# A twelve-stage transformer kernel on one core: six steps of lead instead of five in the last attention, and an earlier context load in the first stage

## The reference

```
# layer 0, attention (the first stage), 4 batches x 16 heads of width 128
x = x + softmax(mask(Q K^T / sqrt(128))) V Wo        # Q, K, V from layernorm(x), with biases
# beside it, for later stages: ternary and int8 versions of weights, and
# the context ctx scaled by its largest absolute value and rounded to fp8

# layer 3, cross attention (the last attention): self and cross heads, 4 x (16 + 16) of width 128
ln = layernorm(layernorm(x)) ; q, k, v = fp8(ln / s) W
q, k = layernorm over each head ("rows") ; P = softmax(q k^T / sqrt(128)) ; o = P v
out = fp8(concat(o) / smooth) Wproj
```

## Time and profile before

| | us |
|---|---|
| median of three runs | 2484.09 (2479.33 to 2488.4) |
| the profiled execution | 2485.58, its span 2483.8 |
| first stage with attention | about 24 to 345 |
| last attention | about 1618 to 2265 |
| mean granted TensorE clock | 0.899 |

### The profile page before, as it was taken

The page is one execution under the profiler, slowest core; times in us unless marked ns, Lnnn a source line. Parts: engine busy times, 40 slices in busy tenths (PEclk is TensorE's granted clock), DMA queues, the critical chain, the costliest instruction groups (busy, mean ns, idle before and its releaser), DMA issues. The chain is left out here.

```text
span 2483.8 us, 38355 instructions
## 1 busy us (share of the span) xinstructions
PE 2070.6 (83%) x13521; PEld 1473.3 (59%) x13521; DVE 1616.2 (65%) x4140; ACT 1109.7 (45%) x2507; POOL 874.7 (35%) x1388
## 2 busy tenths in 40 slices
PE   6898966798798469995559899959999999997991
PEld 4787843465464235553236576637878877785671
DVE  3775657444455945564757897858888888876333
ACT  2256642232342533432754755425555555553330
POOL 2147752112111311111000000046766767764444
PEclk9999987798898568997579999979999999998996
DMA  6014430000000030000000000041111111106553
GB/s 250 25 67 141 148 121 1 1 2 2 1 1 1 27 147 2 1 2 36 1 0 1 1 1 1 1 163 40 55 39 39 56 39 39 48 31 225 111 138 103
DMA packets 57693, 130.96 MB, mean 53 GB/s; under 512 B 6656, under 2 KB 23552, under 8 KB 55520
## 3 DMA queue, kind: packets, MB, share of 16 engines
q1 hardware_dynamic: 52656, 115.80, 13.6%
q0 software_dynamic: 4560, 12.46, 2.3%
q10 hardware_dynamic: 288, 0.26, 0.0%
HBM read 100.31 MB, written 26.08 MB: 51 GB/s over the span
## 5 line engine op out<-in xcount | busy, mean ns | idle before, releaser
L1270 ACT ACTIVATE K<-ps 128x768 f32<-128x768 f32 (+1 forms) x128 | 110.5, 864 | 164.7 <-PE ps L1086 162.9
L2792 POOL TENSOR_TENSOR K<-K 128x512 f32<-128x512 f32 x128 | 134.5, 1050 | 138.5 <-DVE K L2589 138.4
L2191 DVE TENSOR_TENSOR_SCAN W<-W,ps 128x512 f32<-128x512 f32 x128 | 155.8, 1217 | 42.0 <-issue 24.5
L2143 PEld LDWEIGHTS ps<-K 128*128 128x128 f32 x1024 | 136.8, 196 | 65.7 <-issue 51.9
L2732 ACT ACTIVATE K<-ps,K 128x256 f32<-128x256 f32 x128 | 60.6, 474 | 243.1 <-DVE K L2573 243.1
L2584 DVE TENSOR_SCALAR K<-ps,K 128x128 f32<-128x128 f32 x384 | 130.9, 403 | 35.1 <-POOL K L2809 34.8
L2143 PE MATMUL ps<-K 128*128 128x128 f32 x1024 | 139.2, 280 | 8.1 <-DVE W L2191 8.1
L1308 POOL CAST K<-K 128x8 bf16<-128x8 f32 x64 | 14.6, 229 | 369.8 <-issue 209.9
L2778 POOL TENSOR_SCALAR K<-K 128x1 f32<-128x1 f32 x16 | 3.6, 224 | 372.6 <-DVE K L2639 369.7
L2162 PE MATMUL ps<-W,C 128*128 128x512 f32 x256 | 133.3, 603 | 0.7 <-DVE W L2199 0.6
L2482 PE MATMUL ps<-K 128*128 128x256 f32 x512 | 131.8, 380 | 0.7 <-ACT K L2751 0.7
(11 more groups left out here) (528 smaller groups left out, 5849.4 us busy)
## 6 DMA issues: line engine op xcount, KB each, us to landing
W<-split_weights SPq DMA_DIRECT2D x32, 768.0 KB, 4.4
split_weights<-W SPq DMA_DIRECT2D x40, 384.0 KB, 2.6
W<-in_m SPq DMA_DIRECT2D x32, 256.0 KB, 4.9
results<-K SPq DMA_DIRECT2D x63, 128.0 KB
W<-split_weights SPq DMA_DIRECT2D x1, 5376.0 KB, 16.7
W<-in_wproj SPq DMA_DIRECT2D x16, 256.0 KB, 3.0
W<-in_m SPq DMA_DIRECT2D x32, 128.0 KB, 5.1
W<-split_weights SPq DMA_DIRECT2D x1, 3072.0 KB, 20.5
```

Source lines behind the costliest of these rows:

```text
L1270: e.activation(to, made, ACT.Exp, scale=self.SCALE).then_inc(*self.up("exp"))
L2143: m = e.matmul(ps[1 + 2 * (n % 2)][:, b * 128:(b + 1) * 128], self.dtuT[h][:, i, b * 128:(b + 1) * 128], self.diag[s % 4][:, b * 128:(b + ...
L2191: e.tensor_tensor_scan(self.st[i % 3], self.a[i % 3], ps[1 + 2 * (i % 2)][:, :], 0.0, ALU.mult, ALU.add).then_inc(*sig.up("m scan"))
L2792: e.tensor_tensor(Pv, Pv, st[:, 4:6].unsqueeze(2).to_broadcast([128, 2, 256]), ALU.mult).then_inc(*sig.up("x scaled"))
```

## The change

In the first stage the context load goes to the head of SP's list, behind the copy L407 ("lane spread") and ahead of the four stores of ternary weights, into the columns 2048 to 4095 of the shared area; SP no longer waits for the int8 weights, and its part is no longer spread over steps. GpSimd, which now writes the scaled context to columns 0 to 2047, takes over that wait. The work behind the fourth lane sum is spread over three steps: the sum in step 9, L332 and the small VectorE operations in step 10, L334 and L407 in step 11.

In the last attention `LEAD` is 6, the first step is -25 instead of -26, a prep tile takes four steps instead of five, and the feed-forward norms start at 94, 102 and 110. The two turns of prep tiles and of feed-forward inputs stand in steps with `s % 4 == 3` (3 and 7 of a batch; 99, 103, 107, 111, 115, 119). Rows of unit `s + 4` are turned in step `s`. So with `s % 4` = 0, 1, 2, 3 the units are `j` = 2, 3, 0, 1, and the rows turned are those of `j` = 0, 1, 2 and none. Loads of Q weights and of the context are issued one step earlier.

```diff
@@ WeightWork.sp
+        d.wait_ge(sig["lane spread"], 1)
+        d.e.dma_start(L[:, 2048:4096], self.g.dram["ctxT"]).then_inc(*sig.up("ctx in", 16))
         for i, (name, _) in enumerate(self.TERNARY):
             d.wait_ge(sig["ternary"], i + 1)
             d.e.dma_start(self.g.tern[name][0], self.dst).then_inc(*sig.up("w ternary", 16))
-        for _ in range(31):
-            yield
-        d.wait_ge(sig["int8 turned"], 4)
-        d.e.dma_start(L[:, 0:2048], self.g.dram["ctxT"]).then_inc(*sig.up("ctx in", 16))
@@ WeightWork.pe
-        for _ in range(6):
+        for _ in range(7):
             yield
         t.wait_ge(sig["lane sum"], 4)
         t.e.transpose(bank[0:1, 0:16], L[0:16, 0:1], C[0:16, 0:16]).then_inc(*sig.up("lane turned"))
+        yield
         t.wait_ge(sig["lane total"], 1)
         t.e.matmul(bank[:, 32:33], L[0:1, 32:160], L[0:1, 1:2]).then_inc(*sig.up("lane turned"))
-        yield
-        yield
@@ WeightWork.dve
             if n == 3:
+                yield
                 v.wait_ge(sig["lane turned"], 1)
...
                 e.memset(L[0:1, 32:160], 1.0).then_inc(*sig.up("lane total"))
+                yield
                 v.wait_ge(sig["lane turned"], 2)
                 e.tensor_copy(g.lane_total, self.bank[:, 32:33]).then_inc(*sig.up("lane spread"))
-            yield
-            yield
+            else:
+                yield
+                yield
@@ WeightWork.pool
-        cv, sv = (L[:, c:c + 2048].rearrange("p (g n) -> p g n", n=128) for c in (0, 2048))
+        cv, sv = (L[:, c:c + 2048].rearrange("p (g n) -> p g n", n=128) for c in (2048, 0))
         p.wait_ge(sig["ctx scale"], 1)
+        p.wait_ge(sig["int8 turned"], 4)
@@ L3Cross
-    FIRST, LEAD, N = -26, 5, 128
-    PREP, FFN = (-26, 0, 32, 64), (94, 101, 108)
+    FIRST, LEAD, N = -25, 6, 128
+    PREP, FFN = (-25, 0, 32, 64), (94, 102, 110)
...
-            order += [("prep", b, ph // 5) for b, ph in self.at(self.PREP, s, 10) if ph % 5 == 3]
-            order += [("ffn", b, ph - 5) for b, ph in self.at(self.FFN, s, 7) if ph >= 5]
-            if 0 <= s + 3 < self.N and (s + 3) % 4 != 3:
-                order.append(("rows", *divmod(s + 3, 4)))
+            order += [("prep", b, ph // 4) for b, ph in self.at(self.PREP, s, 8) if ph % 4 == 3]
+            order += [("ffn", b, (ph - 5) // 4) for b, ph in self.at(self.FFN, s, 10) if ph in (5, 9)]
+            u = s + self.LEAD - 2
+            if 0 <= u < self.N and u % 4 != 3:
+                order.append(("rows", *divmod(u, 4)))
```

More of the change, by code:

```diff
@@ L441, in dve @@
             yield
-        cv = L[:, 0:2048].rearrange("p (g n) -> p g n", n=128)
+        cv = L[:, 2048:4096].rearrange("p (g n) -> p g n", n=128)
         am, rc = self.f_am, self.f_rc
@@ L465, in dve @@
         for c in range(0, 2048, 512):
-            chain_round_fp8(v, g.ctxq[:, c:c + 512], L[:, 2048 + c:2560 + c], self.f_tmp, self.f_sum)
+            chain_round_fp8(v, g.ctxq[:, c:c + 512], L[:, c:c + 512], self.f_tmp, self.f_sum)
             yield
@@ L559, in sp @@
     def sp(self, d):
-        work = self.work.sp(d)
+        self.work.sp(d)
         for s in range(-self.LEAD, self.N + 30):
             self.split.sp(d, s)
-            if s >= 3:
-                next(work, None)
     def pe(self, t):
@@ L2415, in sp @@
             for G in range(self.N // 4):
-                if s == max(4 * G - 10, self.FIRST):
+                if s == max(4 * G - 11, self.FIRST):
                     d.wait_ge(sig["x unit"], 4 * G - 5)
@@ L2420, in sp @@
             for b in range(B):
-                if s == max(32 * b - 36, self.FIRST):
+                if s == max(32 * b - 37, self.FIRST):
                     d.wait_ge(sig["x unit"], 32 * (b - 1))
@@ L2443, in pe @@
         for s in range(self.FIRST, self.N + 7):
[L2444 to L2447, removed]
+            for b, ph in self.at(self.PREP, s, 8):
+                if ph % 4 == 3:
+                    i = 2 * b + ph // 4
+                    t.wait_ge(sig["x kept"], self.number["prep", b, ph // 4])
                     t.wait_ge(sig["x normed"], i + 1)
@@ L2451, in pe @@
                     m.then_inc(*sig.up("x turned"))
[L2452 to L2455, removed]
+            for b, ph in self.at(self.FFN, s, 10):
+                if ph in (5, 9):
+                    i = (ph - 5) // 4
+                    t.wait_ge(sig["x kept"], self.number["ffn", b, i])
+                    t.wait_ge(sig["f normed"], 2 * b + i + 1)
                     for k in range(2):
-                        m = e.transpose(ps[5][:, k * 128:(k + 1) * 128], self.Y[ph - 5][:, k * 128:(k + 1) * 128], g.ident)
+                        m = e.transpose(ps[5][:, k * 128:(k + 1) * 128], self.Y[i][:, k * 128:(k + 1) * 128], g.ident)
                     m.then_inc(*sig.up("x turned"))
@@ L2560, in dve @@
         for s in range(self.FIRST, self.N + 7):
-            for b, ph in self.at(self.PREP, s, 30):
-                if ph < 10:
-                    self.prep_norm(v, 2 * b + ph // 5, ph % 5)
+            for b, ph in self.at(self.PREP, s, 28):
+                if ph < 8:
+                    self.prep_norm(v, 2 * b + ph // 4, ph % 4)
                 else:
-                    self.prep_round(v, 4 * b + (ph - 10) // 5, self.ORDER[(ph - 10) // 5], (ph - 10) % 5)
+                    self.prep_round(v, 4 * b + (ph - 8) // 5, self.ORDER[(ph - 8) // 5], (ph - 8) % 5)
             for b, ph in self.at(self.FFN, s, 4):
@@ L2698, in act @@
         for s in range(self.FIRST, self.N + 7):
-            for b, ph in self.at(self.PREP, s, 30):
-                if ph in (3, 8):
-                    i, u = ph // 5, self.number["prep", b, ph // 5]
+            for b, ph in self.at(self.PREP, s, 28):
+                if ph in (3, 7):
+                    i, u = ph // 4, self.number["prep", b, ph // 4]
                     a.wait_ge(sig["x turned"], u + 1)
@@ L2711, in act @@
                     e.nop().then_inc(*sig.up("x ln"))
-            for b, ph in self.at(self.FFN, s, 7):
+            for b, ph in self.at(self.FFN, s, 10):
                 if ph == 2:
@@ L2719, in act @@
                                      accum_out=self.st2[:, NT + i, 0:1]).then_inc(*sig.up("f squares"))
-                elif ph >= 5:
-                    i, u = 2 * b + ph - 5, self.number["ffn", b, ph - 5]
+                elif ph in (5, 9):
+                    i, u = 2 * b + (ph - 5) // 4, self.number["ffn", b, (ph - 5) // 4]
                     a.wait_ge(sig["x turned"], u + 1)
@@ L2772, in pool @@
         for s in range(self.FIRST, self.N + 7):
[L2773 to L2777, removed]
+            for b, ph in self.at(self.PREP, s, 28):
+                if ph < 8 and ph % 4 < 2:
+                    i = 2 * b + ph // 4
+                    u = i + NT * (ph % 4)
+                    p.wait_ge(sig["n moments"], 2 * i + ph % 4 + 1)
                     p.step(e.tensor_scalar(rs2[:, u:u + 1], mv2[:, u, 1:2], 1e-5, None, ALU.add).then_inc(p.own, 1))
@@ L2780, in pool @@
                     e.tensor_tensor(rs2[:, u:u + 1], rs2[:, u:u + 1], g.mhalf, ALU.pow).then_inc(*sig.up("n rstd"))
-                elif ph >= 10 and ph % 5 == 2:
-                    n = 4 * b + (ph - 10) // 5
+                elif ph >= 8 and (ph - 8) % 5 == 2:
+                    n = 4 * b + (ph - 8) // 5
                     p.wait_ge(sig["n half"], n + 1)
```

## The result

The changed kernel takes 2465.2 us in the median of six runs (2458.91 to 2476.4), against 2484.09 us for the kernel before: a ratio of 0.9929 with a 95% interval of 0.9909 to 0.9949, so 13 to 23 us less. The forecast was 2467.0. Its profiled execution took 2462.89, with a span of 2461.0 where it was 2483.8.

A forecast was written before the change was run, and what follows sets the result against it. TensorE was taken to bound both changed stages, so only its idle or slow time could be won. First stage -14.7 and last attention -2.4 gave -17.1 us: 2467.0 from the median 2484.1, range 2460 to 2474.

The forecast's parts named there:

- What bounds it: Both changed stages: TensorE sets the pace, its work stays the same, so only its idle or slow time can be won.
- The lane sum: First stage, steps 9 to 11: step 10 runs beside VectorE's fourth sum, a wait of about 1.1 us stays; 6.3 us saved.
- The clock: First stage, behind the lane sum's remaining wait: a lower clock might cost 1.7 us, kept as bound; nothing taken.
- The context: First stage, output product to step 36's turn of probabilities: earlier load covers the reduction, 11.1 us become 2.7; 8.4 saved.
- (a): Last attention: scores' waits for rows of j = 2 turned just before, ten times, all go; 7.6 us saved.
- (b): Last attention: tile and feed-forward turns wait for the bank's keeping, 12 x 1.1 = 13.2 us, 2.2 more than before.
- (c): Last attention: projections wait for VectorE's late rows, two or three times in each of four batches; 2.0 us lost, bounds 0 and 4.
- a sign of being wrong: Last attention: waits for VectorE's rows (L2584) exceeding 4 us would show the prediction wrong.
- (d): End of the last attention: one more short step has no projection to cover its softmax; 1.0 us lost, bounds 0 and 2.
- The run-in: Last attention before the first scores: one more projection in idle time against a later softmax; 0 taken, bounds -1.9 and +3.
- that in which the last attention gains all: Rival: turns wait 0.80, no rows late, run-in gains; last attention -10.9 us, total -25.6, 2458.5 us; 8 in 100.

The follow-up runs named there:

- work_four: Changed kernel with the first stage's weight work (lane sums, context and all behind them) one step later on every engine: 2470.3 us, 0.9938 of the kernel before.
- first_only: Kernel before with the first stage's part of the change alone, last attention as before: 2474.1 us, ratio 0.9949.
- ctx_only: Kernel before with the context loaded sooner alone, lane sums and last attention as before: 2478.5 us, ratio 0.9981.
- five_moved: Changed kernel with rows five steps ahead as before, tile and feed-forward turns in steps that follow one without rows: 2463.7 us, 0.9916 of the kernel before.
- lead_only: Changed kernel with rows six steps ahead, but tile and feed-forward turns in their former steps: 2468.3 us, 0.9934 of the kernel before.
- turns_end: Changed kernel with tile and feed-forward turns (but for the run-in) at the end of the steps without rows: 2457.0 us (0.9893), again 2451.0 (0.9874).
- turns_later: Changed kernel with tile and feed-forward turns (but for the run-in) one step later, behind the step without rows: 2456.3 us, 0.9875 of the kernel before.

## Why the prediction was right, point by point

**What bounds it.** TensorE sets the pace, and in the first stage the gain was its idle and slow time, as forecast. In the last attention that is half the truth: 3.3 of the 5.8 us came out of what the profile counts as busy time at a granted clock of 1.00, which the prediction took as fixed (see the sum).

**The lane sum, 6.3.** The two starts of step 12 (97.33 and 88.36), less the 2.5 that were there before, give 6.46. Alone it gave the same up to step 12, and 5.9 in the stage. The wait was forecast at 1.1 and measured at 1.11.

**The clock.** I let the row on the 1.89 us pause speak for a possible cost of 1.7 us, and took none. No cost came: in the nine profiled executions with the changed lane step (work_four apart, which has no wait there) the wait is 1.11 us and the granted clock behind it 1.00, at full 2.4 GHz. The size of the bound was exact all the same, as the last section shows.

**The context, 8.4.** Up to the turn of step 36 it gave 8.40. The other 0.7 of the stage lay in a small pause (0.74 at 249 us before) that the changed kernel's execution doesn't have and others of the same code do. Alone, 9.3.

**(a) The scores' waits, 7.6.** Right: none is left, and with five steps they are there whatever the turns do (first_only, ctx_only and five_moved).

**(b) The turns, +2.2.** Right in the mechanism: the keeping of the rows just turned is what they wait for, twelve times. The size was off: I took 1.1 a turn and 13.2 in all, and the waits read 0.87 each (twice 1.3) and 11.3 in all, 0.3 more than before and not 2.2. By the length of a group a turn does cost 1.07, but so measured those of before cost more than their 11.0 too.

**(c) Late rows, +2.0.** Wrong, in the place and in the reason; that the size came near is luck. The prediction had rows late two or three times in each of four batches. Behind step 6 no projection waits for them (in the kernel before one did, 0.4 us in step 103). There is +3.4 us instead in the first steps (5.7 for 2.3), where I had put nothing, and 5.7 is over the 4 us that the prediction had named as a sign of being wrong. The reasoning counted what TensorE's steps lose before the tight place and left out what VectorE gains. The instruction that masks the exponent in rounding a pair is the piece that differs most, here in the lines of lead_only (six steps, turns as before) and then of five_moved (five steps, turns moved), with busy us and mean ns:

```profile
L2627 DVE TENSOR_SCALAR K<-K 128x512 int16<-128x512 int16 x60 | 18.8, 313 | 2.1
```

```profile
L2628 DVE TENSOR_SCALAR K<-K 128x512 int16<-128x512 int16 x60 | 38.2, 636 | 2.1
```

With five steps ahead nearly every second one starts 0.14 us after GpSimd's multiplication of the scores and takes as long as that:

```profile
1736.70 1.04 POOL L2793 TENSOR_TENSOR K<-K 128x512 f32<-128x512 f32 x1 [1.56 <-DVE K L2590]
1736.84 1.05 DVE L2628 TENSOR_SCALAR K<-K 128x512 int16<-128x512 int16 x1
```

With six it falls beside something else and takes 0.30. In every kernel with five steps the mean is 0.64 to 0.66, in every one with six 0.31 to 0.34: some 20 us of VectorE's time, bought by the lead and not by the turns. Half of it is paid by GpSimd: the 128 multiplications take 134.5 us in every kernel with five steps and 143.3 to 145.3 in those with six. That all this is why the rows are in time is argued, not shown by a run of its own.

**(d) The tail, +1.0.** It was 0.3 (3.1 us of waits at the turn of probabilities for 2.8). **The run-in, 0:** 32.1 us for 31.8.

**The sum.** -17.1 forecast; by stages -15.5, -5.8, -0.4 between them and +1.5 in the last stage, -20.2 in all; by the medians -18.9. The total came nearer to the forecast than the last attention did, which gave 5.8 for 2.4, and that is in part luck. The stretch from step 0 to the first matmul of the last stage, before and after:

```profile
1654.94:2266.49 611.55, 585.84 (x3677) 475.27 (x3677) 494.84 (x1765) 339.61 (x922) 415.50 (x522) 1.00 0.16 52
1636.82:2242.28 605.46, 582.50 (x3671) 472.28 (x3669) 475.02 (x1763) 348.55 (x922) 411.79 (x522) 1.00 0.16 52
```

TensorE is idle there for 23.0 us in place of 25.7 and busy for 582.5 in place of 585.8, and the run-in is 0.3 longer: -2.7, -3.3 and +0.3. So idle time alone came near the forecast's -2.4, though made up otherwise: -6.7 at the scores (their wait in step 0 counts to the run-in), +0.3 at the turns, +3.4 at late rows, +0.3 at the tail. The 3.3 us of busy time are what the prediction left out. A wait that costs more than its idle row, as in turns_end (1.09 for 0.87), may be the reason; no run shows it for these. No rival took place: that in which the last attention gains all needed turns that wait 0.80, and these came near (0.87), but not the gain in the run-in.

## What to carry to other kernels

Before an exchange of a resource is moved "where there is room", ask who used the resource last in the step before, not in the same step: a turn at the head of a step without rows waited for the rows of the step ahead of it, and the same turn at the end of that step was free, for 12.8 us. Price such a wait by the length of a group with and without it; the idle rows showed four fifths of it. And read what a shift does to the pairing of VectorE and GpSimd: the same code one step apart had 20 us less of VectorE's busy time and 10 us more of GpSimd's.

## What the runs showed of the hardware

**The same pause, two clocks.** The pause of 1.89 us near 55 us was followed by a lower granted clock in eight of the twelve profiled executions that have it, and by 1.00 in four; over the 13 us ahead of it TensorE's idle times are the same in all twelve. The 4.1 us behind it, in the changed kernel and in turns_later (length, busy PE, PEld, DVE, ACT, POOL, granted clock, DMA):

```profile
54.42:58.52 4.10, 4.10 (x15) 3.48 (x16) 2.03 (x6) 2.32 (x8) 1.67 (x2) 0.68 0.03 4
```

```profile
53.23:57.33 4.10, 4.10 (x21) 3.64 (x22) 2.79 (x8) 2.32 (x8) 2.08 (x2) 1.00 0.07 12
```

From the pause to the lane turn it is 28.55 to 28.59 us in the eight and 26.88 us in each of the four: 1.7 us, the bound I had for the clock. A pause of 1.11 us was never followed by it, one of 4.14 always (behind it 0.50, the lower level of 1.2 GHz, in all three profiled executions that have it). The Trainium skill (TensorE: Matmul & The Clock Gate, "HAM oscillation") holds a long pause responsible. The runs agree for 4.14 and 1.11 us; for 1.89 us either may follow, and neither the rule nor the one row of before tells which.

**Stages with the same code scatter through the clock.** In the stage of class L1Cross the changed kernel and turns_end run the same code. The stretches 24 to 32 us behind the stage's start, first of the changed kernel, then of turns_end:

```profile
629.11:633.11 4.00, 3.07 (x9) 1.95 (x7) 0.00 (x0) 1.66 (x4) 0.00 (x0) 0.57 0.00 0
633.11:637.11 4.00, 3.79 (x34) 2.46 (x34) 3.09 (x5) 0.84 (x2) 0.00 (x0) 1.00 0.00 0
```

```profile
627.57:631.57 4.00, 3.07 (x9) 1.83 (x7) 0.00 (x0) 1.66 (x4) 0.00 (x0) 0.55 0.00 0
631.57:635.57 4.00, 4.00 (x20) 2.17 (x21) 2.10 (x3) 0.84 (x2) 0.00 (x0) 0.50 0.00 0
```

The clock returns in one and stays down in the other, and the stage is 191.2 us long in the one, 194.8 in the other, up to 198.1 in a third. The last attention, where the mean granted clock from step 0 on rounds to 1.00 in every execution, repeats better: 637.6 to 637.8 us in three executions, 624.8 twice, 643.4 to 643.7 in the three with the code of before. Even there it isn't safe. The fourth with that code, first_only, took 645.0: TensorE idles 2.66 us ahead of the turn of step 3 in all four, and in this one alone the clock fell. The same 5 us, first_only and before:

```profile
1664.00:1669.00 5.00, 3.35 (x14) 2.58 (x15) 1.32 (x4) 2.59 (x7) 1.04 (x1) 0.66 0.00 2
```

```profile
1667.47:1672.47 5.00, 3.36 (x25) 2.99 (x26) 1.56 (x6) 3.68 (x11) 1.04 (x1) 1.00 0.00 2
```

So differences of a few us between two kernels are read from a stage's length with its granted clock beside it, not from two spans.
